# Second layer of a four-layer graph kernel: gathers in 13 kept parts of 8 rows, a first visit that writes TensorE's banks, and ScalarE's two one-hot steps interleaved

## What is computed

```python
edge_index = jnp.stack([src, dst])
h = jnp.maximum(_layernorm(x, axis=-1), 0.0)
x = x + _L0_gnn_ref(h, edge_index, L0_gnn_W, L0_gnn_a)
h = jnp.maximum(_layernorm(x, axis=-1), 0.0)
x = x + _L1_gnn_ref(h, src, dst, edge_weight)      # the second layer
...
def weighted_midpoint_spmm(x_hyp, c, rows, cols, vals):    # rows = src, cols = dst
    gamma = 2.0 / jnp.clip(1.0 - c * jnp.sum(x_hyp * x_hyp, axis=-1, keepdims=True), EPS)
    gx = gamma * x_hyp
    num = segment_sum(vals[:, None] * gx[cols], rows, num_segments=N_NODES)
    den = segment_sum(vals * (gamma[:, 0] - 1.0)[cols], rows, num_segments=N_NODES)[:, None]
```

## Time and profile before

| what | value |
|---|---|
| median of 3 runs | 4653.99 us (4649.1 to 4656.62) |
| span of the profiled execution, the only time that it has | 4657.2 us |
| TensorE, busy in the span | 1697.7 us (36%) |
| VectorE | 2833.9 us (61%) |
| ScalarE | 1748.2 us (38%) |
| GpSimd | 1878.2 us (40%) |
| share of the second layer's changed stage | 2116 to 2897 us, 781 us |

### The profile page before, as it was taken

One profiled execution on the slowest core, in us unless ns is written; L12 is line 12 of the kernel. 1 busy time (PEld: TensorE's weight loads), 2 busy tenths in 40 slices (PEclk: granted clock), 3 DMA queues, 4 the chain that ended last, 5 costly groups with the idle time before them and its releaser, 6 DMA issues. The chain is left out here.

```text
span 4657.2 us, 47765 instructions
## 1 busy us (share of the span) xinstructions
PE 1697.7 (36%) x10711; PEld 958.0 (21%) x10711; DVE 2833.9 (61%) x4928; ACT 1748.2 (38%) x4626; POOL 1878.2 (40%) x1844
## 2 busy tenths in 40 slices
PE   3162111100000000006666332322222179899989
PEld 2142111100000000001221110111111168444444
DVE  5837599873777779884554333657777757422131
ACT  1334311102565658335665433234444355010011
POOL 0044555556777720024555553277767340000000
PEclk6576555555555555555655666655555589999999
DMA  3000000016666620001222222277778445767845
GB/s 131 14 19 1 3 1 1 1 58 181 175 185 178 183 55 0 0 14 37 63 63 72 63 64 60 97 227 243 241 230 256 114 131 146 293 241 268 281 157 204
DMA packets 215391, 553.46 MB, mean 119 GB/s; under 512 B 46178, under 2 KB 112412, under 8 KB 214405
## 3 DMA queue, kind: packets, MB, share of 16 engines
q0 software_dynamic: 99984, 272.83, 20.7%
q1 hardware_dynamic: 115188, 278.18, 17.3%
HBM read 485.70 MB, written 65.20 MB: 118 GB/s over the span
## 5 line engine op out<-in xcount | busy, mean ns | idle before, releaser
L2829 PE MATMUL fourth_bank<-fourth_tile,fourth_z 128*128 128x512 f16 (+1 forms) x2800 | 559.6, 361 | 19.7 <-DVEq L2990 10.1
L1320 POOL DMA_INDIRECT blend_got<-rec,blend_slot x416 | 401.7, 966 | 365.7 <-DMA blend_got<-rec,blend_slot 252.0
L2191 POOL DMA_INDIRECT heads_got<-rec,heads_slot x416 | 467.6, 1124 | 185.4 <-issue 123.6
L1724 POOL DMA_INDIRECT sum_got<-rec,sum_slot x416 | 451.9, 1086 | 164.9 <-issue 127.5
L1044 POOL DMA_INDIRECT table<-edges_record,edges_place x391 | 393.0, 1005 | 292.3 <-DMA table<-edges_record,edges_place 186.2
L258 PE MATMUL blend_count<-blend_mov,blend_stat 128*128 x980 | 366.7, 473 | 326.8 <-DVE blend_mov L1372 180.0
L214 PE MATMUL edges_p_key<-kept_ident,edges_key_row 128*128 128x128 f32 x4 | 1.1, 428 | 1024.8 <-DVEq L176 1024.8
L1798 DVE TENSOR_TENSOR first_y<-first_y,sum_got 128x516 f32 x416 | 290.8, 699 | 126.5 <-issue 33.5
L1372 DVE TENSOR_SCALAR blend_mov<-built_iota_low,built_low 128x800 f16 x490 | 217.0, 444 | 210.6 <-issue 103.9
L2829 PEld LDWEIGHTS fourth_bank<-fourth_tile,fourth_z 128*128 128x128 f16 x2800 | 261.6, 99 | 311.4 <-issue 14.7
L2304 DVE TENSOR_TENSOR third_a_y<-third_a_y,heads_got 128x520 f32 x416 | 287.8, 692 | 55.9 <-issue 41.5
(11 more groups left out here) (675 smaller groups left out, 4471.1 us busy)
## 6 DMA issues: line engine op xcount, KB each, us to landing
fourth_tile<-cs SPq DMA_DIRECT2D x100, 800.0 KB, 4.5
fourth_tile<-ct SPq DMA_DIRECT2D x100, 800.0 KB, 4.3
ct<-blend_cst SPq DMA_DIRECT2D x20, 1000.0 KB
heads_counts<-ct SPq DMA_DIRECT2D x25, 800.0 KB
cs<-heads_flipped SPq DMA_DIRECT2D x25, 800.0 KB
attend_cnt<-ct SPq DMA_DIRECT2D x50, 256.0 KB
sort_low_wide<-low SPq DMA_DIRECT2D x4, 3136.0 KB
attend_cnt<-ct SPq DMA_DIRECT2D x25, 288.0 KB
```

The costliest lines, as they stand in the source:

```text
L1320: pool.indirect_dma_start(got[:, buf, r, :], None, rec_dram, bass.IndirectOffsetOnAxis(ap=slot[:, t:t + 1], axis=0)).then_inc(gathered[t % ...
L1724: pool.indirect_dma_start(got[:, t % (HELD * PART), :], None, rec_dram, bass.IndirectOffsetOnAxis(ap=slot[:, t:t + 1], axis=0)).then_inc(g ...
L2191: pool.indirect_dma_start(got[:, buf, r, :], None, rec_dram, bass.IndirectOffsetOnAxis(ap=slot[:, t:t + 1], axis=0)).then_inc(gathered[buf ...
L2829: last = pe.matmul(bank[m][:, 0:w], z2[s % 2][:, k, part, :], tile[:, n % RING, at:at + w], start=(k == 0 and part == 0), stop=(k == NB - ...
```

## The change

**Gathers.** `got` still has 104 rows, now as 13 parts of 8 rows, each with its own semaphore. POOL no longer waits for landings. From row 104 on it waits, every 8 rows, until VectorE has added the 8 rows that stood in the part. VectorE waits for landings of 8 rows instead of 26.

**VectorE's order.** The rows lag three blocks: blocks 0 to 2 have none, and 13 rows are added behind the last block.

**TensorE.** The clears and the closing matmul of each block are gone. A block's first visit is written out ahead of the loop, its matmuls write the banks instead of adding to them, and the loop goes over the other tiles; this is why each block has at least two. TensorE waits for `stat_ready` alone.

**ScalarE.** In the turn of visit n it waits for `mov_ready` of visit n, makes `gap` of visit n, and then `stat` of visit n-1. So `stat` of a block's last visit is made in the first turn of the next block. `take` waits for `slot_free` of the block's last visit.

The core of the diff:

```diff
-            step(dve.tensor_scalar(span[:, :, 0], first[:, :], float(ET - 1), None, ALU.min))
-            step(dve.tensor_tensor(last[:, :], last[:, :], span[:, :, 0], ALU.max))
+            step(dve.tensor_scalar(span[:, :, 0], first[:, :], float(ET - 2), None, ALU.min))
+            step(dve.scalar_tensor_tensor(last[:, :], span[:, :, 0], 1.0, last[:, :], ALU.add, ALU.max))
...
-    BUFS, ROWS = 4, 26
+    PART, PARTS_KEPT, LAG = 8, 13, 3
+    KEPT = PART * PARTS_KEPT
...
-            for n in range(SETS):
-                buf = n % BUFS
-                if n >= BUFS:
-                    pool.wait_ge(free[buf], n // BUFS)
-                for r in range(ROWS):
-                    t = n * ROWS + r
-                    if t % IN_FLIGHT == 0 and t:
-                        wait_landed(pool, gathered, t)
+            for t in range(SLOT_ROWS):
+                part = t // PART
+                if t % PART == 0 and part >= PARTS_KEPT:
+                    pool.wait_ge(added, (part - PARTS_KEPT + 1) * PART)
...
-                if r == 0:
-                    wait_landed(dve, gathered, (n + 1) * ROWS)
+                if t % PART == 0:
+                    dve.wait_ge(gathered[part % PARTS_KEPT], 16 * PART * (part // PARTS_KEPT + 1))
...
+            def rows_by(b):
+                return max(0, b - LAG) * SLOT_ROWS // BLOCKS
...
-                act.wait_ge(sum_ready, b + 1)
+                act.wait_ge(slot_free, act.snap(visits[b % 2], min_val=1, max_val=BLOCKS * ET) + RING)
...
+            def narrow_of_the_last(n):
+                before = act.snap((n + RING - 1) % RING, min_val=0, max_val=RING - 1)
+                act.wait_ge(gap_ready, n + 1)
+                act.activation(at_slot(stat, before), at_slot(gap, before), ACT.Relu, bias=1.0, scale=-1.0).then_inc(stat_ready, 1)
...
-                    act.wait_ge(slot_free, n + 1)
+                    act.wait_ge(mov_ready, n + 1)
                     act.activation(at_slot(gap, at), ids, ACT.Abs, bias=K["offset"][:, b // GROUP, bass.ds(t, 1)]).then_inc(gap_ready, 1)
-                    act.wait_ge(gap_ready, n + 1)
-                    act.activation(at_slot(stat, at), at_slot(gap, at), ACT.Relu, bias=1.0, scale=-1.0).then_inc(stat_ready, 1)
+                    narrow_of_the_last(n)
...
+            def visit(banks, first):
+                n, at = slot_of(pe, used)
+                pe.wait_ge(stat_ready, n + 2)
+                moving = at_slot(mov, at)
+                pe.matmul(banks[0], at_slot(stat, at), moving[:, 0:IL // 2], start=first, stop=True, skip_group_check=True)
+                pe.matmul(banks[1], at_slot(stat, at), moving[:, IL // 2:IL], start=first, stop=True, skip_group_check=True).then_inc(slot_free, 1)
+                pe.reg_add(used, used, 1)
...
-                for out in banks:
-                    clear(pe, K, out, IL // 2)
-                with pe.Fori(*tiles_of(pe, tiles, b)):
...
-                add_product(pe, banks[0][:, 0:2], K["zero"][:, 0:P], K["zero"][:, 0:2]).then_inc(sum_ready, 1)
+                first, end = tiles_of(pe, tiles, b)
+                visit(banks, True)
+                with pe.Fori(first + 1, end):
+                    visit(banks, False)
```

More of the change, by code:

```diff
@@ L1287, in blend_and_count @@
     loaded, v, turned, sought, ready, counting = (c.sem(n) for n in ("loaded", "v", "turned", "sought", "ready", "counting"))
-    gathered, free = c.lanes("gathered"), [c.sem(f"free{k}") for k in range(BUFS)]
+    gathered = [c.gather_sem(f"gathered{k}") for k in range(PARTS_KEPT)]
     mov_ready, gap_ready, stat_ready, slot_free = c.sem("mov_ready"), c.sem("gap_ready"), c.sem("stat_ready"), c.sem("slot_free")
-    sum_ready, sum_free = c.sem("sum_ready"), c.sem("sum_free")
+    sum_free = c.sem("sum_free")
     saved, added = [c.sem("saved0"), c.sem("saved1")], c.sem("added")
@@ L1345, in _ @@
             tiles = range_registers(dve)
-            regs = [dve.alloc_register(f"row_chunk{k}") for k in range(BATCH)]
+            regs = [dve.alloc_register(f"row_chunk{k}") for k in range(PART)]
             def add_row(t):
-                n, r = t // ROWS, t % ROWS
-                buf = n % BUFS
-                if r == 0:
-                    wait_landed(dve, gathered, (n + 1) * ROWS)
-                if t % BATCH == 0:
-                    dve.reg_load(regs, chunk_row[0:1, t:t + BATCH])
-                at_chunk = dve.snap(regs[t % BATCH], min_val=0, max_val=NB - 1)
+                part = t // PART
+                if t % PART == 0:
+                    dve.wait_ge(gathered[part % PARTS_KEPT], 16 * PART * (part // PARTS_KEPT + 1))
+                    dve.reg_load(regs, chunk_row[0:1, t:t + PART])
+                at_chunk = dve.snap(regs[t % PART], min_val=0, max_val=NB - 1)
                 out = sums[:, t % 2, bass.ds(at_chunk, 1), :].rearrange("p a f -> p (a f)")
@@ L1359, in add_row @@
                     dve.wait_ge(added, t - 1)
-                dve.scalar_tensor_tensor(out, got[:, buf, r, :], weight[:, t:t + 1], out, ALU.mult, ALU.add).then_inc(added, 1)
-                if r == ROWS - 1:
-                    dve.wait_ge(added, t + 1)
-                    dve.sem_inc(free[buf], 1)
+                dve.scalar_tensor_tensor(out, got[:, t % KEPT, :], weight[:, t:t + 1], out, ALU.mult, ALU.add).then_inc(added, 1)
+            def rows_by(b):
+                return max(0, b - LAG) * SLOT_ROWS // BLOCKS
             for b in range(BLOCKS):
@@ L1373, in _ @@
                     dve.reg_add(made, made, 1)
-                for t in range(b * SLOT_ROWS // BLOCKS, (b + 1) * SLOT_ROWS // BLOCKS):
+                for t in range(rows_by(b), rows_by(b + 1)):
                     add_row(t)
+            for t in range(rows_by(BLOCKS), SLOT_ROWS):
+                add_row(t)
+            dve.wait_ge(added, SLOT_ROWS)
         @block.scalar
@@ L1379, in _ @@
             act.preload_act_table(ACT.Relu)
+            act.copy(at_slot(gap, RING - 1), K["zero"][:, 0:P]).then_inc(gap_ready, 1)
             matched = counter(act, "matched")
+            visits = [counter(act, f"visits{k}") for k in range(2)]
             tiles = range_registers(act)
@@ L1398, in _ @@
                     n, at = slot_of(act, matched)
-                    act.wait_ge(slot_free, n + 1)
+                    act.wait_ge(mov_ready, n + 1)
                     act.activation(at_slot(gap, at), ids, ACT.Abs, bias=K["offset"][:, b // GROUP, bass.ds(t, 1)]).then_inc(gap_ready, 1)
-                    act.wait_ge(gap_ready, n + 1)
-                    act.activation(at_slot(stat, at), at_slot(gap, at), ACT.Relu, bias=1.0, scale=-1.0).then_inc(stat_ready, 1)
+                    narrow_of_the_last(n)
                     act.reg_add(matched, matched, 1)
+                act.reg_mov(visits[b % 2], matched)
                 if b >= 1:
                     take(b - 1)
+            narrow_of_the_last(act.snap(matched, min_val=1, max_val=BLOCKS * ET))
             take(BLOCKS - 1)
@@ L1425, in _ @@
                 banks = [count[b % BANKS][:, k * BANK:k * BANK + IL // 2] for k in range(2)]
-                for out in banks:
-                    clear(pe, K, out, IL // 2)
-                with pe.Fori(*tiles_of(pe, tiles, b)):
-                    n, at = slot_of(pe, used)
-                    pe.wait_ge(mov_ready, n + 1)
-                    pe.wait_ge(stat_ready, n + 1)
-                    moving = at_slot(mov, at)
-                    add_product(pe, banks[0], at_slot(stat, at), moving[:, 0:IL // 2])
-                    add_product(pe, banks[1], at_slot(stat, at), moving[:, IL // 2:IL]).then_inc(slot_free, 1)
-                    pe.reg_add(used, used, 1)
-                add_product(pe, banks[0][:, 0:2], K["zero"][:, 0:P], K["zero"][:, 0:2]).then_inc(sum_ready, 1)
+                first, end = tiles_of(pe, tiles, b)
+                visit(banks, True)
+                with pe.Fori(first + 1, end):
+                    visit(banks, False)
         @block.sync
```

8 lines of the change are left out of this document (3 added, 5 removed).

## The result

The changed kernel takes 4727.7 us in the median of 4 runs (4716.7 to 4749.2), the kernel before beside it 4651.6 us. The ratio is 1.0154 [1.0131, 1.0177], so the kernel is 1.5% slower, where 4436 us and faster were forecast. The profiled execution has a span of 4747.3 us; it is the longest of the four.

What follows compares the result with a forecast made beforehand. Waits were taken to bound the stage: gathers in its last stretch, visits ahead of it. Work of 504 us plus 50 us of pauses ended it 219 us earlier; 4657.2 - 219 + 1 = 4439, forecast as 4436 us, range 4402 to 4495.

Steps and rivals of the forecast that it cites:

- POOL, 1.25 us a gather: POOL in the changed stage: without waits for landings a gather costs 1.25 us, 416 of them 520 us.
- TensorE 0.90, ScalarE 0.75, VectorE 0.6 and 1.33, loads of ranges: 504 us: Changed stage: us per visit, VectorE's 1.33 per block's rows, range loads 4.5; the slowest engine per stretch sums to 504 us.
- rival d: ScalarE's two steps don't overlap, a visit stays at 0.99 us: 4490 to 4514 us, chance 0.12.
- No wait of VectorE for landings: VectorE's row additions: POOL's lead of some 95 rows lasts, so no wait for landed gathers is left.
- Is POOL ever held by the 104 kept rows?: POOL's gathers against the row buffer: issue runs just under the limit, 112 rows at block 9, 104 + 24 allowed.
- To this come irregular pauses ... I add a tenth, 50 us: Changed stage: all sequencers stand for about a microsecond at times; a tenth, 50 us, added to 504 us.
- the 0.02 for slower: The whole kernel: the chance given to its becoming slower by more than can be told from no change.
- Rival (c): Gathers slow down once many are in flight, 1.46 us each, 609 us: 4490 us; 0.12 together with the port rule.
- Rival (e): Waits between ScalarE, TensorE and VectorE make the engines take turns, 13.2 us a block: near 5190 us, chance 0.02.
- The page's rule: VectorE's fast-mode one-hots lock a port, each gather could take 1.69 us: near 4580 us, given 1 in 100.
- rival (b): Pauses and loadings hide in the ring's slack and POOL's gathers bound the stage: 4401 to 4415 us, chance 0.15.

Runs made afterwards that it cites:

- e18: The changed kernel itself, unaltered, run on a chip where the kernel before takes 4565.0 us: 4319.2 us, ratio 0.9460.
- e4: The changed kernel without the second layer's 416 gathers, VectorE adding zeros in their place: 4407.7 us, ratio 0.947, one run.
- e2: The kernel before with POOL's part of the change alone (part semaphores, no wait for landings): 4775.0 us, ratio 1.0268.
- e5: The changed kernel with a fill of 384 columns between two gathers, one gather each 1.74 us: 4608.9 us, ratio 0.9893.

## Why the prediction was wrong

By its own steps:

- **POOL, 1.25 us a gather.** Right wherever POOL isn't held: 80 in 100 us in the result's run. In e18 it took 2621.5 - 2094.0 = 527.5 us from the first gather to the last, against 520 forecast.
- **TensorE 0.90, ScalarE 0.75, VectorE 0.6 and 1.33, loads of ranges: 504 us.** Right where no pause falls: 2643.1 - 2129.3 = 513.8 us in e4, 2615.8 - 2100.3 = 515.5 us in e18, both from TensorE's first matmul to the last take. That ScalarE's steps overlap (against rival d) is part of it: e18's first 100 us above hold 228 matmuls, 114 visits of 0.88 us.
- **No wait of VectorE for landings.** Not tested by the result's run, where the additions themselves were late. In e18 it was wrong at the end: two waits, 17.5 us, one of them 13.6 us for the last eight rows, which could be added 10.5 us after the last gather's issue where some 2.3 us were reckoned.
- **Is POOL ever held by the 104 kept rows?** The answer, just under the limit, held in e18 (4.3 us of waiting, 14 times). In the result's run POOL stood 258 us, 36 times, as the additions were late. This followed from the pauses and didn't cause them: e2, with the additions in their old place, has the same.
- **To this come irregular pauses ... I add a tenth, 50 us.** This is the step that failed. I took them for a fixed share of the work, and measured that share in the earlier trace rows while POOL waited 2.3 us after each fourth gather. They belong to gathers that follow one another closely, and the change quickens just that. What they cost in the result's run is about 846.5 - 515.5 = 331 us, e18 being the same kernel without them, against 50 forecast. The sign was in a row that the prediction used: TensorE's wait instruction, 51 ns in the median, had one of 727.
- **Rivals.** None named it, so the 0.02 for slower was not given for the right reason. Rival (c) had gathers slowed by one another; their duration is unchanged, 939/945/1146 ns against the earlier trace rows. Rival (e) had the right sign with another mechanism, the coupling of the engines: e2 loses without it, and e4, e5 and e18 keep it and lose nothing.
- **The page's rule.** The Trainium skill, "SBUF — State Buffer", in its note on the trap that VectorE blocks DMA, says that GpSimd can't write descriptors while VectorE runs an operation in a two-port fast mode. Whether these one-hots run in that mode no run shows, and it isn't what happened: the gathers aren't held up (939/945/1146 ns), the others stand while they are issued.

Why slower and not merely no faster: the waits for landings, which the earlier trace rows showed as idle time worth taking away, also kept POOL from issuing more than four gathers in 7 us. With them gone, the first 104 gathers come without a break. The first 200 us of the stage hold (30 + 133)/2 = 82 visits, 74 us of work at 0.90: some 120 us are lost. Afterwards VectorE's lateness paces POOL in groups of eight, and pauses go on more thinly until the last gather at 2885.7 us; the other 210 us are lost there.

On the chips without pauses the forecast's parts hold, but what came of them is its rival (b), to which it gave 0.15: TensorE, ScalarE and VectorE's one-hots were done first, and the gathers ended the stage. The last take of e18 began at 2615.8 us; VectorE's last eight additions stood for their gathers until 2632:

```profile
2631.98 2.20 DVE L1354 SCALAR_TENSOR_TENSOR second_sums<-blend_got,blend_weight,second_sums 128x129 f32 x8 [13.56 <-DMA blend_got<-rec,blend_slot]
```

The saving there, 4565.0 - 4319.2 = 246 us, lies between the 239 and 253 us of (b) (4654 less 4415 and 4401), where the forecast had 4654 - 4436 = 218.

What stays open is the cause proper: why a sequencer's own register operation should take 0.7 us when another engine issues indirect DMAs, why in steps of 0.7 us, what of a gather does it, its bytes or its issuing, and what a chip has or hasn't that decides it.

## What to carry to other kernels

Before a wait is taken from an engine that issues indirect DMAs, look at the other engines' sequencer rows in the same stretch (register operations and branches, their median and longest): some of 0.7 us among those of 0.05 say that the wait was also a brake, and a faster issue will multiply them. In such a stretch, space the gathers evenly rather than free them or hold them in groups: a fill of 128 columns between gathers gave 0.971 and 0.968 on the two kinds of chip, where the free version gave 1.010 to 1.015 and 0.946; so it costs some 2% where no pauses come. Compare a candidate on more than one chip before a small loss or a large gain is believed.

## What the runs showed that was not expected

- On chips of one kind, sequencer instructions of TensorE, ScalarE and VectorE took 0.69 to 0.73 us, or about 1.4, in place of 0.04 to 0.2, while GpSimd issued a gather each 1.25 us; at an even 1.74 us none did.
- It isn't confined to this stage. In the later stage that turns the counts, where GpSimd gathers too, TensorE's transposes stand idle with "issue" in the result's run and not at all in e18 (first the former):

```profile
L2238 PE MATMUL heads_p_own<-heads_ident,heads_counts 128*128 128x128 f16 x625 | 110.6, 268 | 63.0 <-issue 62.9
L2238 PE MATMUL heads_p_own<-heads_ident,heads_counts 128*128 128x128 f16 x625 | 99.7, 268 | 0.0
```

- The same program took 4565 us on four chips, within 0.5 us of each other in the median, and 4632, 4652 and 4657 us in the three other groups. The pauses are a candidate for these 67 to 92 us; the kernel before left no trace from a chip without them, so this was not shown. Most of it need not lie in the changed stage: beside e18, the kernel before took 2122.6 - 2100.3 = 22 us longer up to TensorE's first visit and (4657.2 - 2896.1) - (4319.6 - 2615.8) = 57 us longer behind the last take, in code that the change leaves alone.
